# Layer 2's mask loads in a graph-attention kernel: four transfers per tile, placed around the transposes, instead of two

## The reference, cut to what matters

```python
q = (x @ Wq + bq).reshape(n, H, C)
k = (x @ Wk + bk).reshape(n, H, C)
v = (x @ Wv + bv).reshape(n, H, C)
alpha = jnp.einsum('ehc,ehc->eh', q[dst], k[src]) / jnp.sqrt(jnp.float32(C))
amax = jax.ops.segment_max(alpha, dst, num_segments=n)
p = jnp.exp(alpha - amax[dst])
denom = jax.ops.segment_sum(p, dst, num_segments=n) + 1e-16
out = jax.ops.segment_sum(p[:, :, None] * v[src], dst, num_segments=n) / denom[:, :, None]
out = out + x @ Ws + bs          # layer 1: heads side by side, then relu; layer 2: mean over heads
...
x = _layernorm(x + layer2(relu(layer1(x))))
```

## Time and profile before

| | |
|---|---|
| three timed runs | 1842.06 us median (1839.79 to 1844.08) |
| the profiled execution | 1843.3 us, its span 1841.3 us, mean granted TensorE clock 0.98 |
| layer 1, attention | about 236 to 1200 us of the span |
| layer 2, attention | about 1308 to 1837 us of the span |
| TensorE busy | 95% of the span |
| VectorE, ScalarE, GpSimd busy | 85%, 69%, 64% |

### The profile page before, as it was taken

One profiled execution on the slowest core, in us unless ns is written; L12 is line 12 of the kernel. 1 busy time (PEld: TensorE's weight loads), 2 busy tenths in 40 slices (PEclk: granted clock), 3 DMA queues, 4 the chain that ended last, 5 costly groups with the idle time before them and its releaser, 6 DMA issues. The chain is left out here.

```text
span 1841.3 us, 45045 instructions
## 1 busy us (share of the span) xinstructions
PE 1742.8 (95%) x15000; PEld 1301.7 (71%) x15000; DVE 1561.1 (85%) x4538; ACT 1262.7 (69%) x2093; POOL 1175.7 (64%) x1464
## 2 busy tenths in 40 slices
PE   3779899999999999999999999989899999999997
PEld 2556567777777777777777777756677777677776
DVE  7999889888888888888888888835798898989896
ACT  4479877777777777777777777732467676667675
POOL 4300056887777776777777777733477777767776
PEclk9799999999999999999999999989899999999999
DMA  6768857776787777778777787582499999989996
GB/s 165 220 189 255 241 129 152 152 155 153 150 163 155 161 153 150 154 159 159 160 153 150 160 158 158 122 233 60 98 172 183 181 180 169 173 175 188 173 184 110
DMA packets 753665, 301.76 MB, mean 164 GB/s; under 512 B 655864, under 2 KB 734076, under 8 KB 750185
## 3 DMA queue, kind: packets, MB, share of 16 engines
q1 hardware_dynamic: 752266, 296.96, 76.9%
q0 software_dynamic: 640, 1.63, 0.3%
q10 hardware_dynamic: 528, 0.26, 0.0%
HBM read 93.63 MB, written 47.83 MB: 77 GB/s over the span
## 5 line engine op out<-in xcount | busy, mean ns | idle before, releaser
L1423 POOL TENSOR_TENSOR prob_parts_l<-prob_l,prob_parts_l 125x512 f16<-125x512 f32 x600 | 720.6, 1232 | 13.4 <-ACT prob_parts_l L1538 13.4
L1529 ACT ACTIVATE prob_l<-prob_l,neg_max_l 125x1024 f32<-125x1024 f32 (+1 forms) x450 | 521.0, 1160 | 6.4 <-DVE neg_max_l L1624 6.1
L1830 PE MATMUL score_l<-room,QT_l 128*128 128x512 f16 (+2 forms) x2100 | 512.2, 353 | 1.4 <-DVE scale_rows L1796 1.2
L1544 ACT CAST probT_l<-transposed_l 128x375 f16<-128x375 f32 x450 | 213.0, 473 | 412.1 <-PE transposed_l L1856 412.1
L1871 PE MATMUL output_l<-V,prob_flipped_l 128*128 128x256 f16 x2400 | 459.9, 273 | 4.1 <-DMA prob_flipped_l<-prob_parts_l 4.1
L1873 PE MATMUL output_l<-V,prob_flipped_l 128*128 128x128 f16 x2400 | 427.9, 219 | 0.0
L1616 DVE CUSTOM_DVE_ANT_0 prob_l<-score_l,mask_even 125x512 f32<-125x512 f32 (+2 forms) x546 | 333.2, 614 | 87.1 <-PE score_l L1830 84.9
L1616 DVE CUSTOM_DVE_ANT_0 prob_l<-score_l,mask_odd 125x512 f32<-125x512 f32 (+2 forms) x504 | 308.2, 613 | 80.9 <-PE score_l L1830 78.7
L1538 ACT CAST prob_parts_l<-prob_l 125x1024 f16<-125x1024 f32 x300 | 309.2, 1032 | 0.1
L1871 PE MATMUL output_l<-V,probT_l 128*128 128x256 f16 x1350 | 272.8, 274 | 3.8 <-DVE probT_l L1629 1.9
L1871 PEld LDWEIGHTS output_l<-V,prob_flipped_l 128*128 128x128 f16 x2400 | 233.8, 97 | 55.5 <-issue 5.4
(11 more groups left out here) (217 smaller groups left out, 2388.4 us busy)
## 6 DMA issues: line engine op xcount, KB each, us to landing
mask_scratch<-log SPq DMA_DIRECT2D x87, 420.0 KB
mask_even<-mask_scratch SPq DMA_DIRECT2D x25, 448.0 KB
mask_odd<-mask_scratch SPq DMA_DIRECT2D x24, 448.0 KB
mask_odd<-mask_scratch SPq DMA_DIRECT2D x12, 896.0 KB
mask_even<-mask_scratch SPq DMA_DIRECT2D x12, 896.0 KB
prob_flipped_l<-prob_parts_l SPq DMA_TRANSPOSE x600, 3.1
hT_scratch<-rowsT_l SPq DMA_DIRECT2D x24, 250.0 KB, 3.5
mask_odd<-mask_scratch SPq DMA_DIRECT2D x12, 471.2 KB
```

What stands on the lines that cost most here:

```text
L1423: pool.tensor_tensor(parts[0:TP, 1, a:b], prob[:, h % 2, a:b], parts[0:TP, 0, a:b], ALU.subtract).then_inc(s_flo, 1)
L1529: act.activation(e, e, ACT.Exp, bias=neg_max[:, h % 2:h % 2 + 1], accum_out=total[:, h % 2, c:c + 1]).then_inc(s_exp, 1)
L1544: act.copy(probT[:, q, 0, 0:n, 0:TP], flipped_in_psum(h, q, n)).then_inc(s_hi, 1)
L1830: last = pe.matmul(score_bank(h, p)[:, 0:b - a], QT[:, h % 2, i, :], KT[:, h, j, a:b], start=n == 0, stop=n == len(PRODUCTS) - 1)
```

## The change

In layer 2 the load of a part is cut in two. Part 0 becomes a load of pieces 0 and 1 and a load of pieces 2 and 3; part 1 becomes a load of pieces 4 and 5 and a load of piece 6. The first of the two stays where the whole load was, ahead of the step's high transposes. The second goes between the high transposes and the low ones. Both raise the same semaphore, so a clear waits for both (`LOADED` is 64 per tile in layer 2, and 32 as before in layer 1). The loads ahead of layer 2's first step are cut in the same way, with nothing put between them. Layer 1 keeps its four loads per tile and their places.

```diff
@@ projections2: the first loads of the odd buffer
-                a, b = FIRST[0][0], CUTS[ND - 1][1]
-                for r0, r1 in ROW_SPLIT:
-                    sp.dma_start(mask[1][r0:r1, a:b], mask_dram[TP + r0:TP + r1, a:b]).then_inc(s_second, 16)
+                for a, b in FIRST[0], (FIRST[1][0], CUTS[ND - 1][1]):
+                    for r0, r1 in ROW_SPLIT:
+                        sp.dma_start(mask[1][r0:r1, a:b], mask_dram[TP + r0:TP + r1, a:b]).then_inc(s_second, 16)
...
-                                dve.wait_ge(s_second, 16 * len(ROW_SPLIT))
+                                dve.wait_ge(s_second, 2 * 16 * len(ROW_SPLIT))
@@ attention
-        MASK_PARTS = [(CUTS[pieces[0]][0], CUTS[pieces[-1]][1]) for pieces in PART_PIECES]
+
+        LOADS = [[pieces] for pieces in PART_PIECES] if layer == 1 else [[pieces[0:2], pieces[2:]] for pieces in PART_PIECES]
+        LOADED = 16 * len(ROW_SPLIT) * layer
...
-                def load_mask(t, parity, j):
-                    a, b = MASK_PARTS[j]
+                def load_mask(t, parity, j, n):
+                    a, b = CUTS[LOADS[j][n][0]][0], CUTS[LOADS[j][n][-1]][1]
...
-                def flips(s, h):
+                def flips(s, h, between=()):
                     wait(sp, s_fv, ND * (s - 1))
                     if layer == 1 and s == 1:
                         sp.wait_ge(s_bound2, 3)
                     for n in range(2):
+                        if n == 1:
+                            for load in between:
+                                load_mask(*load)
                         for half in range(len(HALVES)):
                             flip(s, h, half, n)
...
-                            load_mask(t + 1 + n, (parity + 1 + n) % 2, j)
+                            loads = [(t + 1 + n, (parity + 1 + n) % 2, j, m) for m in range(len(LOADS[j]))]
+                            load_mask(*loads[0])
+                        else:
+                            loads = ()
                         tn, hn = ahead(t, h, 1)
                         if exists(tn):
-                            flips(s + 1, hn)
+                            flips(s + 1, hn, loads[1:])
...
-                for j in range(0 if layer == 1 else 1, H):
-                    load_mask(1, 1, j)
+                for j in range(0 if layer == 1 else 1, H):
+                    for m in range(len(LOADS[j])):
+                        load_mask(1, 1, j, m)
...
-                    dve.wait_ge(s_mask[t % 2][j], 16 * len(ROW_SPLIT) * ((t + 1) // 2))
+                    dve.wait_ge(s_mask[t % 2][j], LOADED * ((t + 1) // 2))
```

## The result

The changed kernel takes 1848.16 us (median of 9 runs, 1845.45 to 1852.13), the kernel before 1841.32 us in the same comparison (9 runs, 1839.79 to 1844.08). The ratio is 1.0038, 95% interval 1.0028 to 1.0048. That is 6.8 us slower; the prediction said 1849 with a sum of +7.

A forecast was written before the change was run, and what follows sets the result against it. TensorE was taken to bound the kernel, VectorE close behind. Late transfers 5.5, late first halves 1.7 and SyncE jitter 1.4 us, less 1.0 saved, gave 7.6, taken as 7: 1850.3 profiled, 1849 median; range 1840.5 to 1860.

The forecast's parts named there:

- Bound by TensorE, VectorE close behind: Layer 2 intervals: TensorE busy for the whole 10.04 us, VectorE for 9.52, so a wait in VectorE's queue matters.
- The high transposes gain nothing but one wait: Layer 2's high transposes land some 3 us earlier, worth only TensorE's one DMA wait, credited 1 us.
- No cost on SyncE, in part 1, in the cut: SyncE's two more issues per interval cost nothing; piece 6 lands by 9.7 us, before its first clear at 10.6.
- Which second halves are late: Part 0, 23 tiles: a share of 0.3 lands after piece 0's clear at 11.12 us, waiting 0.8 to 0.9 us.
- Landings are late somewhat more often than packets, so I take 0.3: Share of late half loads, raised from layer 1, where 9 of 46 loads had a packet left at 3.85 us.
- the 5 to 10 that I wanted to see: Tiles in which the changed profile would show VectorE idle for a mask DMA before the clear of piece 0.
- late issues in one tile of four: SyncE's issue jitter of half a microsecond, charged as 23 x 0.25 x 0.25 = 1.4 us.
- The estimate of 4.6 us for a landing: Half load from issue to landing: 6.23 + 4.6 = 10.8 us, 0.3 us ahead of piece 0's clear.
- What a wait costs: VectorE's wait before the clear delays scores and `low_part` for TensorE; taken one for one, bounds zero and about twice.
- I take one for one: Each VectorE wait at the clear lengthens the interval equally, since one late clear of 0.13 us cost 0.12.
- upper bound of twice the wait: Most a VectorE wait could cost, since clears meeting GpSimd's subtractions take 1.44 us instead of 0.68.
- The sum: Layer 2's 23 part 0 tiles: 5.5 + 1.7 + 1.4 = 8.6, less 1.0 saved, 7.6 us, taken as 7.

The follow-up runs named there:

- Own semaphores: Changed kernel, same transfers and order, but clears of pieces 0 and 1 wait for the first half alone; 1840.35 us, ratio 0.9998 to the kernel before.
- part 1 only: Changed kernel with only part 1 cut and piece 6 moved between transposes, part 0 loaded whole and first; 1841.63 us, ratio 1.0000 to the kernel before.
- both ahead: Changed kernel with loads still cut and one semaphore, but both halves ahead of the high transposes; 1841.10 us, ratio 0.9996 to the kernel before.
- whole load between: Changed kernel with neither part cut, part 0's one load between high and low transposes, part 1's first; 1907.37 us, ratio 1.0357 to the kernel before.
- part 0 only: Changed kernel with only part 0 cut and its second half moved between transposes, part 1 loaded whole; 1848.97 us, ratio 1.0038 to the kernel before.
- swapped halves: Changed kernel with a semaphore per half, pieces 2 and 3 loaded first, 0 and 1 between transposes; 1850.78 us, ratio 1.0054 to the kernel before.
- later clear: Changed kernel, same transfers, with the clear of piece 0 one slot later on VectorE; 1840.39 us, ratio 0.9996 to the kernel before.

## Why the prediction was right, and where its terms were off

The direction, the place and the size came out, and the own-semaphore pair shows the mechanism. Two terms were mis-sized in opposite directions, and the total owes its fit partly to that.

- *Bound by TensorE, VectorE close behind.* Right. The interval without a wait is unchanged at 10.04 us.
- *The high transposes gain nothing but one wait.* Right. The two landed 2.1 and 2.5 us earlier in the median (7.74 and 8.71 us into the interval instead of 9.80 and 11.19), where I had some 3, and nobody waited for them. The interval at 1535, 1.12 us too long before, lost its wait for a transpose. Own semaphores has these early transposes without the waits, and at 0.9998 their worth is too small to be measured.
- *No cost on SyncE, in part 1, in the cut.* Right, by own semaphores, part 1 only and both ahead, but for one tile in which piece 6 was late.
- *Which second halves are late.* This was the step "Landings are late somewhat more often than packets, so I take 0.3". There are 18 late ones among the 23 tiles, not 7 or the 5 to 10 that I wanted to see. They are of two kinds. Eleven were issued on time, 6.2 to 6.5 us into the interval, and took 5.1 to 6.5 us to land. In layer 1 of the kernel before 13 of 46 loads of this size took more than 5 us, which is the 0.3, so the frequency of layer 1 did not hold in layer 2. Why, these runs do not tell. The other seven took only 4.6 to 4.9 us but were issued 0.7 to 1.9 us late, as in the tile of 1409.27, where the second half went out 7.7 us into the interval:

```profile
1402.60 3.69 SPq L1355 DMA_TRANSPOSE prob_flipped_l<-prob_parts_l  x2
1406.35 0.58 SPq L1341 DMA_DIRECT2D mask_even<-mask_scratch  x1
```

These seven make 5.0 of the 9.5 us. My sum had late issues in one tile of four, but at 0.25 us each. The estimate of 4.6 us for a landing left 0.3 us to spare, and a margin so thin should not have been given a frequency from another layer. The waits are shorter than I had them: 0.5 us in the mean (9.5 over 18) instead of 0.8.
- *What a wait costs.* "I take one for one" was right for the 0.13 us on which it rested and wrong as a law. In the changed kernel a wait that ends the clear 0.70 us late lengthens the interval by 0.32, in seven tiles alike (0.31 to 0.32). The one at 1729.79, which idles 0.92 us, is longer by 0.62, and the one at 1792.80, with 1.02 us, by 0.73. The one at 1409.27, with hardly more, 1.08 us, is longer by 1.57. There a later clear falls into GpSimd's subtractions:

```profile
1414.76 1.35 DVE L1611 SCALAR_TENSOR_TENSOR mask_even<-mask_even 125x512 f32<-125x512 f32 x1
```

```profile
1414.41 5.40 POOL L1432 TENSOR_TENSOR prob_parts_l<-prob_l,prob_parts_l 125x512 f16<-125x512 f32 x4
```

In a tile without a wait that clear takes 0.70 us, and in the one at 1792.80 0.69. So part of a short wait is absorbed, and one of just over a microsecond can grow. Over all, 9.5 us of waits cost 7.0. The whole load between shows growth at a larger size. My upper bound of twice the wait held. That GpSimd's instruction holds the clear back is read from instructions that lie side by side. Two tiles with the same idle time of 0.44 us bear it out, each with the clear and then GpSimd's addition:

```profile
1668.12 0.86 DVE L1611 SCALAR_TENSOR_TENSOR mask_even<-mask_even 125x512 f32<-125x512 f32 x1 [0.44 <-DMA mask_even<-mask_scratch]
...
1667.98 0.46 POOL L1450 TENSOR_TENSOR rows_l<-summed_l,skip_l 125x128 f32<-125x128 f32 x1
```

```profile
1752.11 0.69 DVE L1611 SCALAR_TENSOR_TENSOR mask_even<-mask_even 125x512 f32<-125x512 f32 x1 [0.44 <-DMA mask_even<-mask_scratch]
...
1752.25 0.87 POOL L1450 TENSOR_TENSOR rows_l<-summed_l,skip_l 125x128 f32<-125x128 f32 x1
```

Whichever starts first keeps its usual length, and the other is stretched. The first interval is 0.32 us longer than 10.04 and the second 0.15. No run took GpSimd's instruction away, so what it costs here is argued and not shown.

- *The sum.* The 23 intervals are together 7.0 us longer than without waits. One interval at 1566 is 0.4 longer, where the clear of piece 4 waited for piece 6, and 1.1 is saved at 1535. That makes 6.3 of the 6.8 measured. The span of the profiled execution grew by 3.1 alone, since two things that have nothing to do with the waits went its way. All that lies ahead of layer 2's attention was 1.15 us shorter. And the first full interval of layer 2 ran at a full clock, where the kernel before had 0.92:

```profile
1316.25:1328.66 12.41, 12.41 (x108) 9.86 (x107) 8.44 (x30) 7.05 (x13) 5.94 (x7) 0.92 0.82 178
```

```profile
1315.09:1325.84 10.75, 10.75 (x103) 8.62 (x102) 8.36 (x29) 7.06 (x13) 5.89 (x7) 1.00 0.99 191
```

It is no effect of the change: part 0 only, as slow as the change, has a granted clock of 0.83 from 1304.99 to 1313.62 us, and swapped halves, slower still, has none below 1.00 at this place.

## What to carry to other kernels

Before a load is moved to a later place in a queue, find its first reader and subtract. If what is left is a few tenths of a microsecond, reckon with a wait in most rounds, and give each half of a cut load its own semaphore, so that a reader waits only for the columns it reads. Transposes that land 2 us earlier are worth nothing where nobody waits for them. A wait on the second busiest engine is neither lost in full nor absorbed in full; what it costs depends on what it then runs into. Where it leaves TensorE idle, look at the granted clock of the stretch behind it as well.

## What the runs showed that I had not expected

The cost of a wait goes in steps. In seven tiles of the changed kernel idle times of 0.3 to 0.6 us gave the same 0.31 to 0.32 us, since the clear ended at the same time in all of them, 1.90 to 1.91 us behind `neg_max`. In six of them it had been stretched beside GpSimd's addition, and in the seventh, with 0.60 us idle, it kept its 0.69. With the whole load between, thirteen waits of 1.83 to 2.80 us all gave 12.84 to 12.87 us. And 54.5 us of waits cost 66 us where each was 1.5 us or more, in part through TensorE's clock.

None of the variants beats the kernel before by more than its interval: the best, own semaphores, both ahead and a later clear, stand at 0.9996 to 0.9998.
